# A decoder layer with experts: gathered rows turned by VectorE instead of TensorE

## The reference

```python
x = x + attention(layernorm(x), Wq, Wk, Wv, Wo)                 # 4 x 1024 x 1024, 16 heads, causal
x = x + cross_mix(layernorm(x), ctx_1024, Wq, bq, Wk, bk)
# experts: E = 64, TOP_K = 8, F_INT = 384, H = 1024
h = layernorm(x).reshape(-1, H)                                 # 4096 tokens
top_val, top_idx = top_k(softmax(h @ gate_weight.T), 8)         # partly rerouted by similarity
order = argsort(rerouted); xs = h[order // 8]                   # 32768 rows, sorted by expert
gate, up = split(ragged_dot(xs, gate_up_proj))
y = ragged_dot(silu(gate) * up, down_proj)
x = x + zeros.at[token].add(y * weight)
```

## Time and profile before

| | |
|---|---|
| median of three runs | 7590.41 us (7587.95 to 7591.87) |
| the profiled execution: its own time, and its span | 7591.9 us, 7591.9 us |
| TensorE busy | 7089.7 us, 93% |
| VectorE, ScalarE, GpSimd busy | 52%, 45%, 24% |
| granted TensorE clock, mean | 0.975 |
| turns of gathered rows on TensorE (L1948) | 2080, in groups of eight |
| dn_lo on GpSimd (L1907) | 384, 1300 ns each |

### The profile page before, as it was taken

The page is one execution under the profiler, slowest core; times in us unless marked ns, Lnnn a source line. Parts: engine busy times, 40 slices in busy tenths (PEclk is TensorE's granted clock), DMA queues, the critical chain, the costliest instruction groups (busy, mean ns, idle before and its releaser), DMA issues.

```text
span 7591.9 us, 118507 instructions
## 1 busy us (share of the span) xinstructions
PE 7089.7 (93%) x37743; PEld 5849.8 (77%) x37744; DVE 3948.7 (52%) x7056; ACT 3419.9 (45%) x6382; POOL 1810.6 (24%) x1602
## 2 busy tenths in 40 slices
PE   7998998998995999992999999999999999999999
PEld 5777777777774787872888888888888888888887
DVE  5666666667664344336454444444444444444444
ACT  4666666666664122211344444444444444444443
POOL 1122122122110000000333333333333333333333
PEclk9999999999997999995999999999999999999999
DMA  2222222222212222221565555665555565566555
GB/s 73 55 66 59 54 65 62 54 64 62 55 50 82 84 64 75 78 70 32 157 182 155 156 159 159 168 180 160 161 163 161 160 166 160 161 163 170 159 158 151
DMA packets 313829, 875.34 MB, mean 115 GB/s; under 512 B 44128, under 2 KB 85600, under 8 KB 313568
## 3 DMA queue, kind: packets, MB, share of 16 engines
q0 software_dynamic: 98928, 365.58, 20.7%
q1 hardware_dynamic: 214640, 506.45, 20.6%
HBM read 614.84 MB, written 206.70 MB: 108 GB/s over the span
## 4 chain that ended last, share of the span: by engine, by line
PE 52%; DVE 0%; DMA 0%; POOL 0%; issue 0%; ACT 0%; DVEq 0%; POOLq 0%; ACTq 0%
PE ps_gu L1928 10%; PE ps_gu L1930 10%; PE ps_gu L1929 10%; PE ps_y L1928 5%; PE ps_y L1930 5%; PE ps_y L1929 5%; PE ps_xe L1948 3%; PE ps_xe L1957 1%; PE ps_l L1937 1%; PE ps_h L2040 0%; DVE logits L2202 0%; DMA out<-y_sup,scatter_s 0%; DMA x_rows<-rows,gather_s 0%; DVE xs_lo L2248 0%; DVE at_hi L2195 0%
## 5 line engine op out<-in xcount | busy, mean ns | idle before, releaser
L1928 PE MATMUL ps_gu<-xs_hi,gu_hi 128*128 128x512 f32 x3072 | 1213.5, 395 | 7.3 <-DVE gu_lo L2287 7.3
L1930 PE MATMUL ps_gu<-xs_hi,gu_lo 128*128 128x512 f32 x3072 | 1207.7, 393 | 0.0
L1929 PE MATMUL ps_gu<-xs_lo,gu_hi 128*128 128x512 f32 x3072 | 1204.8, 392 | 0.0
L1907 POOL TENSOR_TENSOR dn_lo<-raw_w,dn_hi 128x512 fp32r<-128x512 f32 x384 | 485.1, 1300 | 945.3 <-ACT dn_hi L2110 945.3
L1928 PEld LDWEIGHTS ps_gu<-xs_hi,gu_hi 128*128 128x128 f32 x3072 | 578.0, 188 | 130.6 <-DVE gu_lo L2287 7.7
L1929 PEld LDWEIGHTS ps_gu<-xs_lo,gu_hi 128*128 128x128 f32 x3072 | 578.2, 188 | 125.2
L1930 PEld LDWEIGHTS ps_gu<-xs_hi,gu_lo 128*128 128x128 f32 x3072 | 577.7, 188 | 125.0
L454 PE MATMUL ps_qkv<-xt_hi,w_hi 128*128 128x512 f32 x1512 | 619.6, 410 | 17.6 <-ACT proj L610 9.9
L1928 PE MATMUL ps_y<-dn_hi,hs_hi 128*128 128x512 f32 x1536 | 628.6, 409 | 0.1
L889 DVE TENSOR_TENSOR pt_lo<-ps_t,pt_hi 128x512 fp32r<-128x512 f32 (+3 forms) x768 | 425.4, 554 | 376.3 <-ACT pt_hi L710 371.6
L454 PE MATMUL ps_qkv<-xt_lo,w_hi 128*128 128x512 f32 x1512 | 609.7, 403 | 0.0
(11 more groups left out here) (325 smaller groups left out, 15534.7 us busy)
## 6 DMA issues: line engine op xcount, KB each, us to landing
raw_w<-w_gu SPq DMA_DIRECT2D x384, 512.0 KB, 4.1
raw_w<-w_down SPq DMA_DIRECT2D x192, 512.0 KB, 6.5
w_raw<-wqkv SPq DMA_DIRECT2D x192, 256.0 KB, 2.6
turned<-proj SPq DMA_DIRECT2D x512, 64.0 KB, 2.0
out<-residual SPq DMA_DIRECT2D x36, 512.0 KB, 2.6
q_hi<-q_hi SPq DMA_DIRECT2D x128, 128.0 KB, 2.3
attn_out<-out_t POOLq DMA_DIRECT2D x128, 128.0 KB, 2.3
residual<-x SPq DMA_DIRECT2D x32, 512.0 KB, 4.6
```

Of the source, the lines that this page charges most:

```text
L1907: pool.tensor_tensor(dn_lo[:, f, a], raw_w[:, f, a], raw(dn_hi[:, f, a]), ALU.subtract).then_inc(dn_lo_ok, 1)
L1928: pe.matmul(out, a_hi, w_hi, start=first, stop=False)
L1929: pe.matmul(out, a_hi, w_lo, start=False, stop=False)
L1930: return pe.matmul(out, a_lo, w_hi, start=False, stop=last)
```

## The change

The gathered rows of the four row blocks are no longer turned by TensorE. For each row block, ScalarE (`move_half`) and VectorE (first part of the new `turn_super`) each copy half of `x_rows` in eight pieces of 32 partitions x 256 elements to another group of 32 partitions of a new tile `pieces`; then VectorE transposes within blocks of 32x32 from `pieces` back into `x_rows`, and `xs_hi` and `xs_lo` are made from there in one instruction each instead of two. Tail rows stay on TensorE.

```diff
+        pieces = m.sb("pieces", [P, 2, Q4, QF])                      # Q4, QF = 4, H // 4
-        row_base = m.sb("row_base", [P, N, N], BF16)
+        row_base = m.sb("row_base", [P, N], BF16)
+        def ps_sup(i):
+            return ps_y if i % 2 else ps_x1
+        def quarter(a, i, q):
+            return x_rows[32 * a:32 * a + 32, i, 0:H].rearrange("p (k q c) -> p k q c", q=Q4, c=32)[:, :, q, :]
...
 # GpSimd, before the gathers of the next expert
-                    pool.wait_ge(xs_ps, START + n * SUP)
+                    pool.wait_ge(xs_lo_ok, START + n * SUP)
...
 # TensorE: turn_super goes; the second layer alternates over ps_xe and ps_y
-                turn_super(e + 1, 0, e + 1 + t0)
-                    turn_super(e + 1, i, e + 1 + t0)
-                turn_tail(e + t0, e + 1)
+                turn_tail(e + t0, e)                                 # now also waits for ys_ok
+                    if f == 0 and i == 0:
+                        pe.wait_ge(xt_lo_ok, START + (e + t0 + 1) * 2)
+                    elif f == 0 and i == 1:
                         pe.wait_ge(yl_ok, START + (e + t0) * 2 + c + 1)
                     elif f == 0:
-                        pe.wait_ge(ys_ok, START + e * 2 * (SUP - 1) + 2 * (i - 1) + c + 1)
+                        pe.wait_ge(ys_ok, START + e * 2 * (SUP - 1) + 2 * (i - 2) + c + 1)
...
 # ScalarE
+            def move_half(n, i, parts=range(Q4)):
+                act.wait_ge(rows_s[i], (n + 1) * 16)
+                if i >= 2 or not (isinstance(n, int) and n == 0):
+                    act.wait_ge(xs_turned, START + n * SUP + i - 1)
+                for q in parts:
+                    for a in range(0, Q4, 2):
+                        mv = act.activation(pieces[32 * q:32 * q + 32, i % 2, a, :].rearrange("p (k c) -> p k c", c=32), quarter(a, i, q), ACT.Copy)
+                if parts[-1] == Q4 - 1:
+                    mv.then_inc(half_moved, 1)
...
                 split(5)
+                move_half(e + 1, 0)
                 silu_of(1)
+                move_half(e + 1, 1)
                 split_h(1)
...
                 silu_of(2)
+                move_half(e + 1, 2)
+                move_half(e + 1, 3, range(2))
                 split_h(2)
+                split_super(e + 1, 0)
+                split_super(e + 1, 1)
+                move_half(e + 1, 3, range(2, Q4))
+                finish(0)
+                split_super(e + 1, 2)
+                finish(1)
+                split_super(e + 1, 3)
+                finish(2)
...
 # VectorE
-                dve.tensor_tensor(at_hi[:, :, 1, :], at_hi[:, :, 1, :], row_base[:, :, :], ALU.mult).then_inc(list_a, 1)
+                dve.tensor_tensor(at_hi[:, :, 1, :], at_hi[:, :, 1, :], row_base[:, :].unsqueeze(2).broadcast_to([P, N, N]), ALU.mult).then_inc(list_a, 1)
-                at = tails_before(dve, n) + n * SUP                  # table of all lists -> of the next four
+            def turn_super(n, i):
+                dve.wait_ge(rows_s[i], (n + 1) * 16)
+                for q in range(Q4):
+                    for a in range(1, Q4, 2):
+                        mv = dve.tensor_copy(pieces[32 * q:32 * q + 32, i % 2, a, :].rearrange("p (k c) -> p k c", c=32), quarter(a, i, q))
+                mv.then_inc(moved, 1)
+                dve.wait_ge(moved, START + n * SUP + i + 1)
+                dve.wait_ge(half_moved, START + n * SUP + i + 1)
+                dve.transpose(x_rows[:, i, 0:H].rearrange("p (k i b) -> p i k b", i=Q4, b=32),
+                              pieces[:, i % 2, :, :].rearrange("p i (k a) -> p i k a", a=32)).then_inc(xs_turned, 1)
...
                 list_part(after, 0)
-                list_part(after, 1)
+                turn_super(e + 1, 0)
                 multiply(1)
                 rest_of_h(1)
                 finish_list(e + AHEAD)
                 keep_tail_weights(e + t0, e)
                 rest_of_tail(e + t0)
+                turn_super(e + 1, 1)
                 # w_last and scatter_l, as before
+                list_part(after, 1)
                 multiply(2)
                 rest_of_h(2)
+                rest_of_super(e + 1, 0)
+                keep_weights(e + 1)
+                turn_super(e + 1, 2)
+                rest_of_super(e + 1, 1)
+                turn_super(e + 1, 3)
+                rest_of_super(e + 1, 2)
+                list_part(after, 2)
+                rest_of_super(e + 1, 3)
+                list_part(after, 3)
+                end_list(after)
```

More of the change, by code:

```diff
@@ L1939, in find_rows, with turn_tail @@
                 mm.then_inc(list_ps, 1)
[L1941 to L1951, removed]
+            def turn_tail(n, e):
                 pe.wait_ge(rows_t, LOADED + (n + 1) * 16)
-                pe.wait_ge(xs_lo_ok, START + supers * 2 * SUP)
                 pe.wait_ge(xt_lo_ok, START + n * 2)
+                pe.wait_ge(ys_ok, START + e * 2 * (SUP - 1))
                 for k in range(HB):
@@ L1958, in turn_tail @@
                 mm.then_inc(xt_ps, 1)
[L1960 to L1963, removed]
+            for n in range(AHEAD):
                 find_rows(n)
@@ L2056, in tail_block @@
                 turn_h(1)
-                turn_tail(e + 1 + t, e + 2)
+                turn_tail(e + 1 + t, e + 1)
                 turn_h(2)
@@ L2148, in super_block, with tail_block @@
                 silu_of(2)
+                move_half(e + 1, 2)
+                move_half(e + 1, 3, range(2))
                 split_h(2)
-                for i in range(SUP):
-                    split_super(e + 1, i)
-                    if i < SUP - 1:
-                        finish(i)
-            def tail_block(e, t):
+                split_super(e + 1, 0)
[6 more added lines that the diff above has]
+                finish(2)
+            def tail_block(e, t, t0):
                 def silu_of(f):
@@ L2224, in finish_list, with gather_super_index @@
                 dve.wait_ge(found_ok, START + n + 1)
-                at = tails_before(dve, n) + n * SUP
-                dve.tensor_tensor(table[:, bass.ds(at + 1, N)], found[:, 0, :], found[:, 1, :], ALU.add).then_inc(list_ok, 1)
+                dve.tensor_tensor(table[:, bass.ds((n & AHEAD) * N, N)], found[:, 0, :], found[:, 1, :], ALU.add).then_inc(list_ok, 1)
                 dve.wait_ge(list_ok, START + n + 1)
-            def gather_super_index(n, tails):
+            def gather_super_index(n):
                 if not (isinstance(n, int) and n == 0):
@@ L2234, in gather_super_index, with nth_block @@
                 stand_alone(dve, passed)
-                dve.tensor_copy(gather_s[:, :], table[:, bass.ds(n * SUP + tails + 1, SUP)]).then_inc(gs_ok, 1)
+                dve.tensor_copy(gather_s[:, :], table[:, bass.ds((n & AHEAD) * N, SUP)]).then_inc(gs_ok, 1)
+            def nth_block(e, i):
+                return ((e & AHEAD) * N + SUP + i) & (LISTS * N - 1)
             def gather_tail_index(n, at):
@@ L2270, in _ @@
             finish_list(0)
-            gather_super_index(0, 0)
+            gather_super_index(0)
             make_list(1)
             keep_weights(0)
+            turn_super(0, 0)
             for i in range(SUP):
+                if i + 1 < SUP:
+                    turn_super(0, i + 1)
                 rest_of_super(0, i)
@@ L2336, in super_block, with tail_block @@
                 dve.tensor_copy(scatter_l[:, :], scatter_s[:, SUP - 1:SUP]).then_inc(sl_ok, 1)
+                list_part(after, 1)
                 multiply(2)
                 rest_of_h(2)
-                for i in range(SUP):
-                    rest_of_super(e + 1, i)
-                    if i == 0:
-                        keep_weights(e + 1)
-                    elif i < SUP - 1:
-                        list_part(after, i + 1)
-                    if i == SUP - 2:
-                        end_list(after)
-            def tail_block(e, t):
+                rest_of_super(e + 1, 0)
[8 more added lines that the diff above has]
+                end_list(after)
+            def tail_block(e, t, t0):
                 def multiply(f):
```

56 lines of the change are left out of this document (29 added, 27 removed).

## The result

The changed kernel takes 7629.3 us (median of 4 runs, 7617.6 to 7641.6), the kernel before 7589.2 beside it (7587.6 to 7591.9). The ratio is 1.0050, with a 95% interval of 1.0036 to 1.0065: by the ratio 38 us slower, 27 to 49. The forecast was 7640, slower. The profiled execution of the changed kernel is at the upper end of its spread (7641.6, span 7640.0), so against the profiled 7591.9 of before there are 48 us to be explained.

A forecast was written before the change was run, and what follows sets the result against it. The prediction took TensorE, busy 500 of 500 us in the experts' stage, as the bound. It summed 53 - 43 + 5 + 35 = +50 us on the profiled 7591.9, giving 7640 us, range 7485 to 7700.

The forecast's parts named there:

- TensorE's lost turns: On TensorE, four row-block turns per expert go: 3.49 us off 55.2, leaving 51.7 us.
- The cost of a copy and a turn: Per row block, VectorE's eight copies take 2.5 us and its turn 1.22; a ScalarE copy takes 0.41 us.
- Rival 3: Copies take 425 ns without port waits, a turn costs 4.8 us; total 7658 us; chance 0.13.
- The first place: At block 1's turn, GpSimd's dn_lo pieces delay three copies; multiply(2) is 2.2 us late, TensorE stands 1.6 us.
- rival 1: VectorE's copies are not held by GpSimd's port, so multiply(2) is on time; total 7501 us; chance 0.2.
- The second place: VectorE's work from multiply(2) makes the next expert's first layer 1.6 us late: +53 us for 33 experts.
- Tail blocks: Where a tail block follows, lost turns outweigh the waits: -1.4 us for each of 31 blocks, -43 us.
- The prologue: Before expert 0 nothing covers the turning: VectorE's 19.6 us replace 14.4, +5 us.
- The clock: New TensorE stalls before 33 first layers lower the granted clock some six times in ten: +35 us.
- The four banks: Second layer over four banks removes TensorE's waits for the emptied bank; worth nothing and costs nothing.

The follow-up runs named there:

- short dn_lo pieces: The changed kernel with GpSimd's six dn_lo subtractions cut from 512 to 8 columns each: 7492.5 us.
- the filler: The changed kernel with ten unread TensorE matmuls added behind the second layer of each expert without a tail: 7587.2 us.
- find_rows late: The changed kernel with VectorE's last list work moved to the next expert's block and find_rows moved behind first_layer(1, 0) on TensorE: 7564.2 us.
- split(6) ahead: The changed kernel with ScalarE's split of the first chunk of the down weights moved ahead of its copies: 7516.6 us.

## Why the prediction was right

The direction, the two places of the wait and the time were forecast. That the time is so close (7640 against 7629.3) is in part luck: two terms of the sum were wrong by 19 and 16 us and cancelled.

**TensorE's lost turns.** The forecast took 3.49 us off each expert and left 51.7. Measured, the work without waits is 56.3 - 1.36 - 2.7 = 52.2, so the term was right within 0.5.

**The cost of a copy and a turn.** VectorE's copy was taken at 294 ns and 2.5 us for eight; 286 ns and 2.39 us were measured. The turn was taken at 1.22 us with no row for it and takes 1.25. ScalarE's copy was taken at 0.41 and takes 0.42, the row_base multiply at 1.22 and takes 1.23. The upper ends, 425 ns and 2.4 us, were not met. Rival 3, which rested on the first, was also summed too low: 35.0 + 0.65 + 21.7 against 55.2 is +2.15 us and not +1.8, which makes 7670 of its 7658.

**The first place.** The forecast had three blocked copies, multiply(2) at T+37.2, 2.2 us late, and TensorE still for 1.6 us. Measured were exactly three, multiply(2) at 3855.26 - 3816.53 - 1.7 = T+37.0, a wait of 1.36. The experiment with short dn_lo pieces shows that this is GpSimd's doing, and rival 1's time, 7501, is that kernel's (7492). The row that decided it was an instruction with two SBUF inputs; that single-input fp32 copies are held too is now shown. The Trainium skill says of the lock, in "SBUF — State Buffer", section "SBUF: two separate sides", that a VectorE instruction takes it in a two-port mode, into which an fp32 copy from SBUF to SBUF goes, or with two SBUF inputs. The held copies (815, 1295 and 1297 ns) and the held start_list (1.22 to 2.32 us) agree with it; which mode the copies ran in no run here shows.

**The second place.** The forecast had 19.2 us of VectorE's order and 0.4 for contention, which put the next first layer at T+56.85. Measured from multiply(2) to the end of the first half of gu_lo: 3873.67 + 0.65 - 3855.26 = 19.06; the 0.4 did not come. With multiply(2) 0.2 us earlier than forecast, the next first layer is at T+56.2. So an undisturbed expert takes 56.3 us: +1.04 and not +1.6 us for 33 experts, 34 us instead of 53. Moving the list work (e.g. to the next block) cut the wait from 94.8 to 34.9 us, which shows that the order on VectorE was its cause; what then remains, 0.95 us each, is ScalarE's, which the forecast had as staying ahead.

**Tail blocks.** The forecast was -1.4 us for each, -43 us. With the clock taken out by the filler it is 68.10 against 69.74, -1.64, which is -49 us for 30. The wait for the tail's gather was forecast at 0.45 in each; measured were 13 waits of together 11.7 us, the longest 2.0.

**The prologue.** The forecast was +5 us. The first expert's start is 10.3 us later. Of these 6.2 stood already when VectorE's first instruction of the experts' stage began (3553.93 against 3547.74), behind code that the change does not touch. From there to the copy that follows the first row gathers it is 27.05 us instead of 28.50, 1.5 less. From that copy to the first matmul, the turning itself, it is 38.3 instead of 32.7: +5.6, so this term was right. The 6.2 us are no part of the change: in the profiled executions of the experiments, all with the same code up to there, that instruction began between 3544.2 and 3564.2.

**The clock.** This term was mis-sized: a loss at six in ten of 33 starts, 1.7 us each, was put at 35 us. It came at 27 of the 33 and once elsewhere, and the filler shows 51 us. The price of one was right (102 us at half clock in 28 drops, 1.8 each), its frequency was not. It was taken from a few stalls of the attention stage, of which two are shown, one with a drop and one without. The trace of the kernel before has 13 TensorE waits of 2.5 to 3.9 us between 500 and 2250 us, and a drop began at eleven of them. Counting them all would have given a frequency near the 27 of 33.

**The four banks.** The forecast put them at nothing, because TensorE did not wait for a bank before. In the changed kernel they hide a ScalarE that is later; taking them away costs some 85 us. The forecast needed no number for this, but its reason held only for the kernel before.

So +34.3 - 49.2 + 51.2 (the clock) + 1.2 (the last expert) + 10.3 make 47.8. The forecast was +50, from +53, -43, +35 and +5. The sum is closer than its terms: the road was 19 us too dear and the clock 16 too cheap, and the 6.2 us that are no part of the change stand against 6 more that the tails gave back. What the prediction lacked was the size of the alternatives. It gave rival 1 the price of an unblocked port correctly (7501 against 7492), but did not say that a line's move on ScalarE would reach nearly all of it.

## What to carry to other kernels

Work taken off the bounding engine becomes a gain only if the other engines' ordered lists are shorter than what remains: add up VectorE's list from the instruction that the bounding engine feeds to the one that feeds it back, and set the sum beside it. When work is added on VectorE, look at which GpSimd instructions stand beside it; the cure may be to start the GpSimd work elsewhere, beside instructions that have slack. Every wait of TensorE that is longer than the 1.36 us seen here without a drop should be priced with the clock loss that may follow, which here was as large as the lateness itself (51 us against 34).

## What the runs showed of the hardware

- A blocked VectorE copy of 286 ns takes as long as one GpSimd piece (1.30 us), and the two engines take turns: three copies in a row were held (815, 1295, 1297 ns), each until a piece ended. bf16 instructions of 1.22 us became 2.32 in the same way, and GpSimd's two pieces 3.81 us instead of 2.6.
- A TensorE wait of 1.36 us alone in an expert went with no drop of the granted clock (filled kernel, 64 waits). One of 1.77 us (up to 2.3) did in 14 experts (find_rows late). One of 2.3 to 2.8 us did in 17 of 33 where no wait for hs_lo stood ahead of it (short dn_lo pieces; split(6) ahead), and in 27 of 33 where one of 1.36 us stood some 15 us ahead of it. With one pair of banks 44 of 64 experts had a drop, 36 of them at two waits of some 1.4 and 1.9 us with 1.7 us of work between them. A drop was 3.41 us, seldom 6.8, at 1.2 GHz. Why it follows some of these waits and not others of the same length stays open.
- The turn on VectorE, 1024 fp32 elements a partition in 32x32 pieces, takes 1.25 us, the same as a two-input instruction of that size. ScalarE's copies of 256 elements from one partition group to another take 0.42 us and do not overlap (eight in 3.4).
